# GpSimd takes group norm scaling, history, scale renewal and a Gelu product from VectorE in a recurrent decoder

## What is computed

```python
def _slstm_layer(xn, cw, cb, wi, wf, wz, wo, rk, b, gnw):
    xc = jax.nn.silu(causal_conv(xn, cw) + cb)             # K = 4 taps
    ...                                                    # wx: gates i, f from xc; z, o from xn
    def step(carry, wx_t):
        h, c, n, m = carry
        raw = wx_t + jnp.einsum('bhd,hdgo->bhgo', h, rk) + b
        ...
        cn = fg * c + ig * jnp.tanh(zr)
        nn = fg * n + ig
        hn = jax.nn.sigmoid(og) * cn / nn
        return ((hn, cn, nn, mn), hn)
    _, ys = lax.scan(step, ...)
    mu = y.mean(-1, keepdims=True)
    var = y.var(-1, keepdims=True)
    y = (y - mu) * lax.rsqrt(var + EPS) * gnw.reshape(H, DH)   # per head: group norm
    return y.reshape(Bc, Sc, Dc)

for l in range(L):
    x = x + _slstm_layer(_ln(x, ln1_w[l]), ...)
    u = _ln(x, ln2_w[l]) @ ff_up[l]
    x = x + (jax.nn.gelu(u[..., :UP], approximate=False) * u[..., UP:]) @ ff_down[l]
```

## Time and profile before

| | us |
|---|---|
| median of 3 runs | 4291.18 (4288.7 to 4295.0) |
| profiled execution, its own time | 4289.6 |
| its span | 4287.7 |
| TensorE busy | 3693.7 (86%) |
| VectorE busy | 3497.4 (82%) |
| ScalarE busy | 2843.3 (66%) |
| GpSimd busy | 1036.9 (24%) |

### The profile page before, as it was taken

How to read it: one execution, slowest core, us unless ns; L and a number is a source line. 1 busy time by engine, 2 the same in 40 slices (tenths; PEclk the granted TensorE clock), 3 DMA queues, 4 the chain that set the end, 5 groups by cost and what they waited for, 6 DMA issues and landing times. The chain is left out here.

```text
span 4287.7 us, 113408 instructions
## 1 busy us (share of the span) xinstructions
PE 3693.7 (86%) x42154; PEld 2230.9 (52%) x42154; DVE 3497.4 (82%) x14953; ACT 2843.3 (66%) x9230; POOL 1036.9 (24%) x1217
## 2 busy tenths in 40 slices
PE   5777777648999999999999999999969999999987
PEld 3433433434555555555555555555534555555655
DVE  7777788778888888888888888888758888888875
ACT  4555566545666666666666666666726888888883
POOL 1000000000000000000000000000007888899983
PEclk6555555557999999999999999999968999999998
DMA  4222222201433333343343333333342213331200
GB/s 100 71 69 72 67 71 82 75 7 27 86 78 76 82 76 79 75 85 78 71 86 80 71 82 74 80 76 82 84 112 65 66 54 80 80 78 50 72 25 25
DMA packets 262085, 305.34 MB, mean 71 GB/s; under 512 B 21752, under 2 KB 255032, under 8 KB 256376
## 3 DMA queue, kind: packets, MB, share of 16 engines
q1 hardware_dynamic: 258356, 293.73, 28.7%
q10 hardware_dynamic: 3176, 4.36, 0.4%
HBM read 241.03 MB, written 55.78 MB: 69 GB/s over the span
## 5 line engine op out<-in xcount | busy, mean ns | idle before, releaser
L1365 PEld LDWEIGHTS G<-st,rec_w 128*128 128x128 f16 x19456 | 611.7, 100 | 807.4 <-DVE st L1551 764.5
L1365 PE MATMUL G<-st,rec_w 128*128 128x1 f16 x19456 | 685.0, 165 | 280.5 <-DVE st L1551 267.2
L1823 POOL TENSOR_TENSOR plt<-pft,pht 128x512 f16<-128x512 f32 x765 | 867.2, 1166 | 153.5 <-DVE pht L2066 82.4
L1315 PE MATMUL OA<-pf,vals 128*97 128x512 f32 (+1 forms) x1632 | 884.8, 625 | 0.7
L1226 ACT ACTIVATE st<-hb 32x16 f16<-32x16 f32 x1216 | 258.8, 213 | 625.9 <-DVE hb L1546 622.3
L153 DVE TENSOR_REDUCE mx<-MB 128x1 f32<-128x512 f32 (+1 forms) x832 | 536.7, 661 | 62.3 <-PE MB L145 54.7
L1207 ACT ACTIVATE pf<-SC,ln_prob 128x512 f32<-128x512 f32 (+1 forms) x816 | 560.9, 687 | 20.6
L153 DVE TENSOR_REDUCE mx<-MT 128x1 f32<-128x512 f32 (+1 forms) x832 | 523.5, 664 | 51.5 <-PE MT L1872 41.2
L1818 ACT ACTIVATE pft<-ST,ln_prob 128x512 f32<-128x512 f32 (+1 forms) x816 | 537.5, 689 | 34.1 <-PE ST L1894 33.6
L1816 ACT ACTIVATE pht<-ST,ln_prob 128x512 f16<-128x512 f32 x510 | 351.5, 689 | 193.9 <-PE ST L1894 188.8
L136 PE MATMUL SC<-q_in,k_in 65*128 65x128 f16 (+1 forms) x3264 | 479.8, 224 | 0.0
(11 more groups left out here) (364 smaller groups left out, 7019.2 us busy)
## 6 DMA issues: line engine op xcount, KB each, us to landing
kc_in<-scr_k SPq DMA_DIRECT2D x384, 256.0 KB, 4.3
k_in<-scr_k SPq DMA_DIRECT2D x192, 256.0 KB, 4.9
vc<-scr_v SPq DMA_DIRECT2D x16, 1644.8 KB, 15.6
kc<-scr_k SPq DMA_DIRECT2D x32, 816.0 KB, 13.2
scr_v<-v_hl SPq DMA_DIRECT2D x24, 1032.0 KB, 5.6
scr_k<-k_hl SPq DMA_DIRECT2D x192, 128.0 KB, 1.7
k<-scr_k SPq DMA_DIRECT2D x16, 816.0 KB, 6.6
kc_in<-scr_k SPq DMA_DIRECT2D x32, 192.0 KB, 3.6
```

The source lines that it names most:

```text
L1315: pe.matmul(OA[0:at.DC + 1, :], at.vals[0:rows, i, :], pf[0:rows, tile % 2, :], start=(i == 0), stop=(i == KT - 1)).then_inc(pv_done, 1)
L1365: mm = pe.matmul(g[:, t, c:c + 1], rec_w[:, c, :], st[:, c:c + 1], start=False, stop=(c == C - 1), skip_group_check=True)
L1823: return eng.tensor_tensor(pl[0:k, t % NP_, :], pf[0:k, t % NP_, :], ph[0:k, t % NP_, :], ALU.subtract)
```

## The change

GpSimd takes over `yc` (now a mean `ymean` and a subtraction), the multiplication by `gn_w`, the one by `rstd` (they change places: `yr` is now `yc` times `gn_w`), `x1`, the history, and `ks`, `rck`, `kap` of the renewal. The polynomial has one factor less on VectorE: ScalarE makes the linear start `gth` = a6 `gs` + a5 in step 11, GpSimd multiplies it by `gs`, and VectorE goes on from there in steps 12 to 14. On GpSimd every item waits for nothing but its inputs (and what is ahead in the queue). `vector_load` is rewritten, so the maxima move.

```diff
         def dve_head_mean(dve, k):
             dve.wait_ge(B["yt"], k)
             nc.vector.tensor_reduce(ysum[:, :], yt[:, :, :], AX_X, ALU.add).then_inc(B["ysum"], 1)
-            dve.wait_ge(B["ysum"], k)
-            nc.vector.scalar_tensor_tensor(out=yc[:, :, :], in0=bc(ysum[:, :], DH), scalar=-1.0 / DH, in1=yt[:, :, :],
-                                           op0=ALU.mult, op1=ALU.add).then_inc(B["yc"], 1)
+
+        def pool_head_center(pool, k):
+            pool.wait_ge(B["ysum"], k)
+            nc.gpsimd.tensor_scalar(ymean[:, :], ysum[:, :], 1.0 / DH, 0.0, ALU.mult, ALU.add).then_inc(B["ymn"], 1)
+            pool.wait_ge(B["ymn"], k)
+            nc.gpsimd.tensor_tensor(yc[:, :, :], yt[:, :, :], bc(ymean[:, :], DH), ALU.subtract).then_inc(B["yc"], 1)
+
+        def pool_head_weight(pool, k):
+            pool.wait_ge(B["yc"], k)
+            nc.gpsimd.tensor_tensor(yr[:, :, :].rearrange("p h o -> p (h o)"), yc[:, :, :].rearrange("p h o -> p (h o)"),
+                                    gn_w[:, :], ALU.mult).then_inc(B["yrr"], 1)
...
-        def dve_head_norm(dve, k):
...
+        def pool_head_norm(pool, k):
+            pool.wait_ge(B["yrr"], k)
+            pool.wait_ge(B["grs"], k)
+            nc.gpsimd.tensor_tensor(yg[:, :].rearrange("p (h o) -> p h o", h=H), yr[:, :, :], bc(rstd[:, :], DH),
                                     ALU.mult).then_inc(B["gnw"], 1)
...
+        def pool_x1(pool, residual, k):
+            pool.wait_ge(B["gnw"], k)
+            nc.gpsimd.tensor_tensor(x1[:, :], residual, yg[:, :], ALU.add).then_inc(B["x1r"], 1)
+
+        def dve_x1(dve, k):
             dve.wait_ge(B["x1r"], k)
             dve_stats(dve, x1[:, :], B["st2"], B["mv2"], k)
...
+        def act_gelu_first(a, k):
+            a.wait_ge(B["gsr"], k)
+            nc.scalar.activation(gth[:, :], gs[:, :], ACT.Identity, bias=gelu_5[:, 0:1], scale=GELU_A[6]).then_inc(B["g1r"], 1)
+
+        def pool_gelu(pool, k):
+            pool.wait_ge(B["g1r"], k)
+            nc.gpsimd.tensor_tensor(gq[:, :], gth[:, :], gs[:, :], ALU.mult).then_inc(B["gqr"], 1)
+
         def dve_gelu(dve, part, k):
...
+            for i in ((1,), (2, 3), (4, 5))[part]:
                 dve.wait_ge(B["gqr"], done + i)
...
                 def _(pool):
+                    def pool_renew(c, k):
+                        m = 8 * (k - 1)
+                        pool.wait_ge(k_ready, m + 5)
+                        g.tensor_tensor(ks[:, :], kap[:, :], kd[:, :], ALU.add).then_inc(k_ready, 1)
+                        g.tensor_tensor(rck[:, :], nlo[:, :], keep_at(slice(0, Q), c), ALU.mult).then_inc(k_ready, 1)
+                        pool.wait_ge(k_ready, m + 7)
+                        g.tensor_tensor(kap[:, :], ks[:, :], keep_at(slice(0, Q), c), ALU.mult).then_inc(k_ready, 1)
...
+                            if t == T_MEAN:
+                                pool_head_center(pool, k)
                             if t == T_VAR:
+                                pool_head_weight(pool, k)
                                 pool_head_scale(pool, k)
+                            if t == T_GN:
+                                pool_head_norm(pool, k)
+                                pool_x1(pool, xin[(p + 1) % 2][:, :], k)
+                            if t == T_GELU:
+                                pool_gelu(pool, k)
+                            if t == T_STAT1 + 1:
+                                history(g, base + p + 1)
+                            if t == T_RENEW[3]:
+                                pool_renew(base + p + 1, k)
...
                             s.activation(st[2 * Q:3 * Q, :], hb[p % 2][:, t, :], ACT.Copy).then_inc(parts_ready, 1)
+                            if t == T_GELU:
+                                act_gelu_first(a, p + 1)
...
-                        if T_GELU <= t < T_GELU + 4:
-                            dve_gelu(dve, t - T_GELU, k)
+                        if T_GELU < t < T_GELU + 4:
+                            dve_gelu(dve, t - T_GELU - 1, k)
...
-        vector_load = [0.4, 0.4, 0.4, 0.4, 0.6, 0.3, 0.6, 0.9, 0, 0.1, 0.4, 0.6, 0.7, 0.7, 0.35, 0.7, 0.1, 0.5, 0.35, 0.32,
-                       0.5, 0.6, 0.4, 1.2, 1.2, 0.6, 0.6, 0.5, 0.15, 0.15, 0.15, 0.3]
+        vector_load = [0.4, 0.4, 0.4, 0.4, 0.3, 0.3, 0.1, 0.6, 0, 0.25, 0.5, 0.1, 0.1, 0.7, 0.7, 0.7, 0.4, 0.55, 0.35, 0.32,
+                       0.5, 0.35, 0.2, 1.2, 1.2, 0.35, 0.45, 0.45, 0.4, 0.4, 0.4, 0.3]
```

More of the change, by code:

```diff
@@ L491, in slstm_stage @@
         ysum = sb("ysum", [P, H])
+        ymean = sb("ymean", [P, H])
+        gelu_5 = sb("gelu_5", [P, 1])
         yvar = sb("yvar", [P, H])
@@ L781, in slstm_stage @@
             "st1 mv1 ve1 rs1 nb1 nm1 tp1 xn1 cvr sgt xcr xap xbp "
-            "yt ysum yc ysq yvar gve grs yrr gnw x1r st2 mv2 ve2 rs2 nb2 nm2 tp2 n2r upr gsr gqr thr glr acr tpa atr dnr x2r"
+            "yt ysum ymn yc ysq yvar gve grs yrr gnw x1r st2 mv2 ve2 rs2 nb2 nm2 tp2 n2r upr gsr g1r gqr thr glr acr tpa atr dnr x2r"
         ).split()}
@@ L836, in act_norm, with history @@
                                  scale=rstd[:, 0:1]).then_inc(B[f"nm{n}"], 1)
-        def dve_history(c):
-            nc.vector.tensor_tensor(xn[:, :, 0:K - 1], xn[:, :, CH:CH + K - 1],
+        def history(engine, c):
+            engine.tensor_tensor(xn[:, :, 0:K - 1], xn[:, :, CH:CH + K - 1],
                                     bc(keep[:, bass.ds(c, 1), 0:C:H].rearrange("p a l -> p (a l)"), K - 1),
@@ L1025, in _ @@
                 dve_stats(dve, xin[0][:, :], B["st1"], B["mv1"], 1)
-                dve_history(0)
+                history(nc.vector, 0)
                 for half in range(2):
@@ L1600, in _ @@
                 act_gelu(a, 1)
+                act_gelu_first(a, 1)
                 act_gelu_tanh(a, 1)
@@ L1618, in _ @@
                 dve_head_var(dve, 1)
-                dve_head_norm(dve, 1)
-                dve_x1(dve, xin[(ITERS - 1) % 2][:, :], 1)
-                for part in range(4):
+                dve_x1(dve, 1)
+                for part in range(3):
                     dve_gelu(dve, part, 1)
```

46 lines of the change are left out of this document (14 added, 32 removed).

## The result

The changed kernel takes 4300.7 us (median of 16 runs, 4297.7 to 4308.3) against 4291.7 (16 runs, 4287.9 to 4297.5): a ratio of 1.0022, 95% interval 1.0015 to 1.0029. It is slower by 9 us. The forecast was 4300, 9 us slower.

A forecast was written before the change was run, and what follows sets the result against it. Every step was taken as a loop through four engines, bounded by VectorE in 383 of 895 steps, TensorE in 262, the bare loop in 250. Terms -21.8 + 10.4 + 20.0 + 1.0 = +9.6 us gave 4300, range 4262 to 4334.

The forecast's parts named there:

- gaps: Time from the end of `st` to the next `uu`: lighter VectorE saves 21.8 us, ScalarE's new activation costs 10.4.
- blocking: GpSimd products stall VectorE operations with two SBUF inputs in the recurrence's chain, `uu` to `st`: +20.0 us, bounds 0 and 45.
- last pass: Pass behind the loop, a plain chain: two hops and slower operations on GpSimd, +1 us.
- one-column products left no mark: In the chain, small GpSimd operations were to block little: together 0.05 us or less a chunk.
- The quarter: Share of the attention stretch's blocking taken as hidden where TensorE is late: 28 x 0.62 x 0.75.
- rival 1: GpSimd doesn't disturb the recurrence's narrow VectorE operations: -10 us, 4281, chance 0.22.
- Rival 4: Blocking lasts the whole GpSimd instruction, small ones too: 82 us in place of 20, 4362, chance 0.05.
- Rival 3: Every moved product meets the recurrence, `uu` starting earlier: +25 us over the sum, 4325, chance 0.17.
- its time less 0.15: How long a GpSimd product blocks VectorE: up to 0.44 - 0.15 = 0.29 us for 128 columns.
- the new placing of maxima: Steps 27 to 31 lose 41 of 164 maxima, 9 us gained; step 12 gets 48 instead of 11.
- The sum of the three maxima: Each step's gap as the largest of bare loop, VectorE's items and TensorE's late work, added over steps: 21.8 us gained.
- ScalarE's floor: Step 11's gap can't be under 1.22 us, as `act_gelu_first` delays the exponential and `tfz`: 7.1 us attention, 3.3 first stretch.

The follow-up runs named there:

- e6: Changed kernel, but GpSimd's `gn_w` product waits for `yvar`, and `yg` and `x1` wait for the last `st` of step 6: 4284.7 us, ratio 0.9989 to before.
- e5: Kernel before plus seven idle GpSimd operations per chunk on tiles nobody else uses, each in its own step: 4289.4 us, one run.
- e1: Changed kernel with the `vector_load` list of the kernel before, nothing else: 4295.0 us, ratio 1.0012 to before.
- e7: e6 with the `vector_load` list of the kernel before: 4276.0 us, ratio 0.9970 to before.
- e9: Kernel before with only the new `vector_load` list: 4324.7 us, ratio 1.0073 to before.
- e4: Changed kernel with the Gelu polynomial back on VectorE and list entries 11, 12 and 14 of before: 4301.6 us, ratio 1.0024 to before.
- e8: e7 with the Gelu polynomial back on VectorE: 4275.1 us, ratio 0.9964 to before.

## Why the prediction came true, and what in it was wrong

**The total.** Forecast: gaps -21.8 + 10.4 = -11.4 us, blocking +20.0, last pass +1.0, together +9.6. The traces: gaps -2.6 in the first stretch and -5.3 in the second, together -7.9; chains +5.1 and +13.0, together +18.1; last pass +1.0 (24.5 against 23.55). The sum is +11.2, and the medians are 9.1 apart. The forecast of 4300 for 4300.7 is closer than its terms were: gaps came out 3.5 us worse and blocking 1.9 us better, and inside both terms larger errors cancel, as follows. That part is luck. The range of 4262 to 4334 was eight times as wide as the change. (The profiled spans are 14.2 apart; 2.8 of it lie in the third stretch outside the last pass, where nothing was changed.)

**Blocking: right in kind, its size by two errors that cancel.** Before hiding I had 0.7 us a chunk in the first stretch and 0.62 in the second; measured are 0.51 and 0.46. `yc` and the weight were to cost 0.40 together in step 5 and cost 0.21 and 0.17; `yg` was to cost 0.25 and cost 0.21 and 0.25 in step 6; `x1` was to cost 0.1 and meets the chain in 7 of 38 chunks only, 0.04 a chunk on average and part of step 6's growth; steps 8, 21 and 22 have 0.03, 0.03 and 0.02 in the first stretch, by the history and `kap` in the last two. In step 8 it is `nmean`, one column, which now starts 0.01 before `uu` and makes it 0.03 longer; before, it started 0.32 behind `uu`. So "one-column products left no mark" doesn't hold in general. All meetings add up to 18.1, where 10 x 0.7 + 28 x 0.62 = 24.4 stood. The quarter that I took to be hidden by a late TensorE brought this down to 20.0. Little of such hiding shows: when e6 takes 14.9 us out of the chains, the gaps right behind grow by 1.9, and in e5 the gap behind step 9 stays at 1.38 where its chain grew by 0.12. e5 shows the mechanism by itself, so rival 1 falls as a mechanism. Rival 4 falls too: under the power nothing is blocked, and a small operation took 0.06 at most, not 0.22. Rival 3 put four meetings of 0.29 in each chunk, 1.16; steps 5 and 6 together have 0.42.

The Trainium skill, "SBUF — State Buffer", section "SBUF: two separate sides", has the lock last for the whole instruction, for whichever begins first, and against GpSimd operations that read SBUF. For the products the trace agrees: a short operation that VectorE begins under one ends 0.02 to 0.05 behind it, or at its usual time if that is later, and what it has begun before isn't held. My "its time less 0.15" is the same thing seen from the other side: what VectorE's operation would have taken anyway is no loss. Whether the memset, which reads nothing, agrees can't be told, since nothing would have ended before it. The power of four columns (1.01 us, it reads eight) doesn't: VectorE's operations run through under it, begun 0.10 us or more behind its start. The prediction read the row of 3326.36 in the earlier trace rows as one with GpSimd idle; in fact a product of GpSimd's ran until 3326.41, 0.05 into it, and cost nothing, as VectorE's operation ended long behind it anyway.

**Gaps: the sum came near (-7.9 for -11.4), the reading of it did not hold.** I wrote that half of the gain is the new placing of maxima. The part that I named did come, 7 us in steps 27 to 31 against the 9 forecast; step 6 went from 1.29 to 1.13; and step 12, named as standing against it, went from 1.00 to 1.49 (forecast 1.04 to 1.55), 13.7 us. I never added up the placing by itself. e1, e7 and e9 do: it costs 17, 13 and 34 us of gaps in the traces, 4, 8.7 and 29 in the runs. What gains is the relief alone: with the old list the gaps of the attention stretch fall from 1069.1 to 1046.9. The sum of the three maxima had this in it. Taken for e9 it gave 26 of the 34 before that ran.

Over the attention stretch the forecast was -12.2, ScalarE's floor included, and the trace has -5.3. The difference of 7, of which up to 5 may be scatter, can't be put to one step, as the prediction gives few of its steps singly. Measured against before, step 12 is 13.7 us longer, 25, 7, 21, 14 and 0 are 3 to 5.4 longer; 16 is 9.1 shorter, 20, 6, 30 and 4 are 3.7 to 4.7 shorter. Which wait does that is open.

**ScalarE.** The floor of 1.22 was wrong. I read "no slack at all" off, where `tfz` starts 0.04 before the exponential ends; behind the new activation it starts 0.11 before, and the gap is mostly 1.09, on average 1.17. In the first stretch step 11 went from 0.89 to 0.99, 1.0 us and not 3.3, as there too `tfz` starts before the copy ahead of it ends. Besides that, step 12 gained 3.5 us there, steps 21 and 26 together 1.0, and step 14 lost 0.7: -2.6 in sum with the small rest, where -2.5 + 3.3 = +0.8 was forecast. e4 and e8 say what the whole Gelu exchange is worth: nothing that the runs show (medians 0.9 apart, once each way); the traces put gaps and chains together 2.4 and 3.1 us lower with it, 1.6 of that in the first stretch both times.

**What was to show it.** `uu`'s wait rose by 39 us (45 forecast). The first stretch rose by 2.5 us, just over the 2 that would have spoken against the blocking: its chains rose by 5.1, as they should, but the gaps fell by 2.6. That test was badly built, on a sum of two effects; the chain alone is the test. `cn` and the first `st` are longer, and `uu` too, but `hb` hardly. ScalarE's wait in front of `tfz` is gone in step 11, as forecast, though the gap is not 1.22; step 12 has become VectorE's. VectorE's busy time fell by 57 us, not by the 91 that leave it: 18.0 of the missing 34 are inside the blocked operations. The rest is a matter of counting: busy time counts a moment once, where VectorE's operations overlap in the trace; added up one by one up to the last `st`, they fall by 73.2, which with 18.0 makes 91.2. The third stretch grew by 3.7 us, 1.0 of it the last pass. GpSimd's durations were close: 0.40 to 0.48 for 128 columns (0.44), 0.54 for 168 (0.51), 0.19 to 0.22 for the small ones.

## What to carry to other kernels

An operation that is moved to GpSimd needs a place as much as a duration: "as soon as its inputs are there" put wide products under the recurrence's chain, and two waits that hold them until VectorE reads PSUM or stands idle took 15 us out of the chains and 14 off the time. When work leaves an engine and the planner's table is rewritten at the same time, price the table by itself on both codes; here it cost what the relief had gained. And move only what the bound steps hold: four of ten operations carried the whole gain.
